# First experts of a two-layer cross-attention and experts kernel: weights of one expert per shared unit, places right behind the choice, unbroken scatters, second product's low halves on VectorE

## Chip, cores and metric
One core of a Trainium2 chip. The metric is device time in microseconds of one launch; the time of before is the median of three runs. One launch was also profiled.

## The reference, cut
x is 16 sequences of 112 tokens of 256 floats. Four steps follow one another: cross-attention of layer 0, the experts of layer 0, cross-attention of layer 1, the experts of layer 1. The change is in the experts of layer 0 alone. With h = layernorm(x), N = 1792 tokens:
```python
gates = softmax(xf @ router_w)                    # 14 experts
top_v, top_i = top_k(gates, 2)
masked = zeros_like(gates).at[arange(N)[:, None], top_i].set(top_v)
masked = masked / (masked.sum(-1, keepdims=True) + EPS)
routed = vmap(_ffn)(rms_w, w1, w2)                # _ffn: silu((rmsnorm(xn)*rw) @ W1) @ W2
shared = vmap(_ffn)(rms_w_s, w1_s, w2_s).sum(0)   # 2 shared experts, for all tokens
x = x + tanh(g_ffn[0]) * (einsum('end,ne->nd', routed, masked) + shared)
```
W1 is 256x512, W2 512x256, float32.

## The kernel before, in words
`build` (L2371) calls the four stages, with a barrier of all engines between them. The stage in question is `l0_experts` (L905). Products in float32 are made of three in bfloat16 (`three_products`, L45): each operand is split into a high half (the cast) and a low half (what the cast lost).

**Units.** The stage runs 57 units (`Unit0`, L890). Units 0 to 15 are shared ones: 8 per shared expert, each with 224 tokens. Units 16 to 56 are 41 blocks of 128 routed tokens. TensorE does for iteration s (from -2): the transposes of block s+2 (`turned`), the first product of unit s+1 (`up`), the second product of unit s (`down`). ScalarE makes the silu from PSUM to `hf` (`silu`, L1184), VectorE the high half `hh` (L1330) and the low half `hl` (L1332) in `halves`, and for shared units the addition to `xs` (`add_shared`, L1334, 2 instructions). `hf` is one buffer: the next silu waits for `h_lo`. `down` waits for `h_lo`.

**Weights.** 16 loads (`LOADS`): the two shared experts, then the 14 routed ones, each of w1 and w2, 512 KB (128x1024 float32) each, through two raw buffers, issued in order on SP (`load`, L988). Load n's w1 waits for the w1 low half of load n-2 (`w1_lo`), its w2 for the w2 low half of load n-2 (`w2_lo`). ScalarE makes the high halves (w1: `split1`, L1152, two instructions with the norm's weight; w2: `high2`, L1161), VectorE w1's low half (`split1`, L1248, two instructions), GpSimd w2's (`split2`, L1023). Load 15 takes the slot of shared expert 0, so it is split when that expert's units are done, in iteration 12, its w2 all on VectorE. Loads 3 to 14 are split in iterations 0 to 5, two in each, behind the unit's work on ScalarE and VectorE.

**Routing.** TensorE makes the logits, VectorE picks the two experts of each token (`choose`, L1272) and, in the same function, the gates. In iteration 3 (`RANK_AT`) TensorE makes ranks (17 matmuls, `ranks`, L1069) and VectorE computes from them each token's place (`place`, L1299, up to `pos_done`) and the expert of each block (`bexp_done`, L1319). GpSimd then issues 32 scatters of 112 rows of 1 KB from `xn` to `xd` in DRAM (L1037). After each five it does the w2 low half of one of loads 9 to 14. SP loads the blocks from `xd` behind all weights and all scatters.

The lines that set this order:
```python
RANK_AT = 3
LAST_AT = 2 * SH - 4
SCATTER_FROM, SCATTERS = 9, 5
...
for n in range(2 * B):
    ...
    if n % SCATTERS == SCATTERS - 1 and ahead:
        split2(ahead.pop(0))
```


## Time and profile before
| | us |
|---|---|
| runs | 1035.86, 1033.06, 1030.75 |
| median | 1033.06 |
| profiled execution, its own time | 1035.79 |
| its span, first to last instruction | 1034.1 |
| busy in it: TensorE, VectorE, ScalarE, GpSimd | 779.9, 629.7, 470.2, 398.8 |
| mean granted TensorE clock | 0.882 of full |

In the rows below PE is TensorE, PEld its weight loads, DVE VectorE, ACT ScalarE, POOL GpSimd, SPq the queue of SyncE. Times are us from the start of the span unless a column is marked otherwise. The same line stands for all calls of a helper: L51 is the matmul of `three_products`. A name on the left of `<-` is written, those on the right are read. "[4.15 <-DVE f_hl L1332]" means that the engine was idle for 4.15 us before and that this instruction of VectorE ended it. "x2" merges two neighbours of the same kind, and the duration is then that of both.

### The profile page before, as it was taken

How to read it: one execution, taken by the hardware profiler on the slowest of the kernel's cores; microseconds unless marked ns; L12 is line 12 of the kernel's file. 1: busy time of each engine (PE TensorE's matmuls, PEld its weight loads, DVE VectorE, ACT ScalarE, POOL GpSimd, SP SyncE). 2: the span in 40 equal slices, each digit the busy share in tenths (PEclk: the TensorE clock that was granted, in tenths of full speed). 3: DMA queues.
4: the chain of work that ended last, by engine and by line, in shares of the span. 5: the costliest groups of instructions: out<-in, count | busy, mean ns of one | idle time of the engine just before them, and what ended most of it. 6: DMA issues, size and time to landing. Idle time of an engine off the chain costs nothing. (4 is left out here: it accounts for less than half of the span.)

```text
span 1034.1 us, 22027 instructions
## 1 busy us (share of the span) xinstructions
PE 779.9 (75%) x7078; PEld 612.3 (59%) x7093; DVE 629.7 (61%) x1486; ACT 470.2 (45%) x974; POOL 398.8 (39%) x423
## 2 busy tenths in 40 slices
PE   4589999998874866269999999447778627999850
PEld 2357677666563766269877777336667614666430
DVE  8567677776638778446433343157687626666766
ACT  3736555565542654312333333134555315776642
POOL 4377233323200236850000000356687342856555
PEclk9889999999977598779999999779788758999985
DMA  5456223222612345530222222528743021422323
GB/s 151 104 135 162 55 62 76 60 68 46 191 44 83 123 127 173 181 125 7 62 63 64 72 63 67 134 78 223 194 136 91 23 61 50 135 77 86 94 82 102
DMA packets 86021, 101.59 MB, mean 98 GB/s; under 512 B 16854, under 2 KB 72710, under 8 KB 85926
## 3 DMA queue, kind: packets, MB, share of 16 engines
q1 hardware_dynamic: 70614, 69.71, 23.4%
q0 software_dynamic: 12272, 28.81, 10.1%
q10 hardware_dynamic: 3040, 1.81, 0.7%
q8 instruction: 59, 0.97, 0.4%
q14 instruction: 36, 0.29, 0.1%
HBM read 61.03 MB, written 24.38 MB: 83 GB/s over the span
## 5 line engine op out<-in xcount | busy, mean ns | idle before, releaser
L640 DVE TENSOR_REDUCE a_mx<-ps 112x2 f32<-112x750 f32 x128 | 119.8, 936 | 43.7 <-PE ps L323 38.6
L51 PE MATMUL ps<-f_w2hi,f_hh 128*128 (+1 forms) x292 | 83.8, 287 | 44.5 <-DVE f_hl L1332 44.5
L1582 POOL DMA_INDIRECT a_yg<-f_yd,pos x32 | 32.9, 1028 | 210.6 <-POOLq L89 202.0
L1330 DVE CAST f_hh<-f_hf 128x512 bf16<-128x512 f32 (+1 forms) x57 | 32.3, 566 | 109.1 <-ACT f_hf L1188 84.4
L529 ACT ACTIVATE a_Pf<-ps 125x672 f32<-125x672 f32 x128 | 89.9, 729 | 17.1 <-PE ps L271 16.3
L51 PE MATMUL ps<-f_w2hi,f_hl 128*128 (+1 forms) x292 | 83.4, 286 | 0.0
L51 PE MATMUL ps<-f_w2lo,f_hh 128*128 (+1 forms) x292 | 83.4, 286 | 0.0
L323 PE MATMUL ps<-a_stkK,a_stkQ 96*112 96x375 bf16 x256 | 68.1, 349 | 19.8 <-DMA a_stkK<-a_KS 10.0
L51 PE MATMUL ps<-f_xgThi,f_w1hi 128*128 128x128 bf16 x328 | 73.7, 227 | 7.5 <-issue 5.0
L51 PE MATMUL ps<-f_xgTlo,f_w1hi 128*128 128x128 bf16 x328 | 70.6, 217 | 0.0
L51 PE MATMUL ps<-f_xgThi,f_w1lo 128*128 128x128 bf16 x328 | 70.3, 217 | 0.2
L546 POOL DMA_DIRECT2D a_stkK<-a_KS x96 | 51.3, 541 | 45.8 <-DVE a_KS L607 28.7
L2177 ACT ACTIVATE f_rf<-ps,f_ln 128x128 f32<-128x128 f32 x136 | 54.4, 451 | 30.2 <-PE ps L2130 30.2
L51 PEld LDWEIGHTS ps<-f_w2hi,f_hh 128*128 128x128 bf16 (+1 forms) x292 | 34.9, 119 | 51.8 <-DVE f_hl L1332 45.5
L540 POOL TENSOR_TENSOR a_ctxL<-a_ctxF,a_ctxH 128x750 bf16<-128x750 f32 x16 | 25.6, 1602 | 102.9 <-ACT a_ctxH L429 102.9
L2231 POOL TENSOR_TENSOR f_rl<-f_rf,f_rh 128x512 bf16<-128x512 f32 x34 | 39.5, 1160 | 66.8 <-DVE f_rh L2299 65.4
L271 PE MATMUL ps<-a_stkQ,a_stkK 98*125 98x224 bf16 (+1 forms) x384 | 61.2, 269 | 2.3 <-DMA a_stkQ<-a_cneg 2.3
L1188 ACT ACTIVATE f_hf<-ps 128x512 f32<-128x512 f32 x41 | 24.5, 597 | 77.1 <-PE ps L51 77.1
L284 PE MATMUL ps<-a_Pf,a_V 125*32 125x112 f32 x1536 | 52.9, 272 | 2.7 <-DVE xn L655 1.0
L323 PEld LDWEIGHTS ps<-a_stkK,a_stkQ 96*112 96x112 bf16 (+1 forms) x256 | 29.8, 133 | 41.7 <-issue 22.1
L271 PEld LDWEIGHTS ps<-a_stkQ,a_stkK 98*125 98x125 bf16 x384 | 47.8, 142 | 9.3 <-DMA a_stkQ<-a_cneg 2.5
L1027 POOL TENSOR_TENSOR f_w2lo<-f_raw,f_w2hi 128x1024 bf16<-128x1024 f32 x15 | 34.8, 2326 | 45.6 <-ACT f_w2hi L1164 45.5
(398 smaller groups left out, 2454.9 us busy)
## 6 DMA issues: line engine op xcount, KB each, us to landing
f_raw<-F_w SPq DMA_DIRECT2D x28, 512.0 KB
f_xg<-f_xd SPq DMA_DIRECT2D x75, 128.0 KB
f_yd<-f_yo SPq DMA_DIRECT2D x75, 128.0 KB
a_ctxF<-ctxT SPq DMA_DIRECT2D x16, 375.0 KB
a_cT<-ctxT SPq DMA_DIRECT2D x16, 375.0 KB
a_cR<-ctx SPq DMA_DIRECT2D x16, 375.0 KB
f_xd<-a_zero POOLq DMA_DIRECT2D x1, 5248.0 KB, 19.8
a_stkK<-a_KS SPq DMA_DIRECT2D x96, 46.9 KB
```

Of the source, the lines that this page charges most:

```text
L51: ins = nc.tensor.matmul(out, l, r, start=first and i == 0, stop=last and i == len(steps) - 1)
L271: last = nc.tensor.matmul(psST[:C, j % 2, c, :QW], stkK[:, b.slot, j // JJ, j % JJ, c * C:(c + 1) * C], stkQ[:, bass.ds(b.b, 1), j // JJ, ...
L284: last = nc.tensor.matmul(psPV[VW * q:VW * (q + 1), :], V[:, b.slot, c, h, :], Pf[:, h // 2 % PB, c, h % 2 * T:(h % 2 + 1) * T], start=c = ...
L323: last = nc.tensor.matmul(psMX[:T, h, :S], stkQ[0:96, bass.ds(n.b, 1), j // JJ, j % JJ, h * T:(h + 1) * T].rearrange("p o q -> p (o q)"), ...
L529: nc.scalar.activation(Pf[:, s % PB], psST[:C, s % 2, :SC, :QW], ACT.Exp).then_inc(exp_done, 1)
L546: pool.dma_start(stkK[32 * a:32 * a + 32, w.slot, :, jj, :], KS[32 * jj:32 * jj + 32, w.odd, part])\
L640: nc.vector.reduce_max(mx[:, n.odd, 2 * j:2 * j + 2], psMX[:T, :, :S], AX).then_inc(mx_red, 1)
L1027: nc.gpsimd.tensor_tensor(w2[1][:, l.slot], raw2[:, i], w2[0][:, l.slot], ALU.subtract).then_inc(w2_lo, 1)
L1330: nc.vector.tensor_copy(hh[:, s.odd, 0:n], hf[:, 0:n]).then_inc(h_hi, 1)
L1582: nc.gpsimd.indirect_dma_start(out=yg[:, i, b, :], out_offset=None, in_=yd, in_offset=bass.IndirectOffsetOnAxis(k.pos[:, i, b:b + 1], 0), ...
L2177: nc.scalar.activation(rf[:, t % 2, i, :], k.ps[:, 2 + t % 2, i * P:(i + 1) * P], ACT.Relu, bias=ln[:, 1, bass.ds(e, 1), i], scale=ln[:, 0 ...
L2231: nc.gpsimd.tensor_tensor(rl[:, t % 2], rf[:, t % 2], rh[:, t % 2], ALU.subtract).then_inc(r_lo, 1)
```

## The change
- Loads 3 to 15 are split one in each of iterations 0 to 12, and not two in each of 0 to 5 and the last in 12.
- `ranks` runs in iteration 0, between `up` of unit 1 and `down` of unit 0. On VectorE gates and places are computed in iteration 0, ahead of unit 1's halves; load 2's w1 low half stands behind them and no longer ahead of the choice. The experts of the blocks are computed in iteration 4, in a function of their own.
- GpSimd makes the w2 low halves of loads 0, 1, 2, 13 and 14; VectorE makes those of loads 3 to 12. The 32 scatters stand in one row, between loads 2 and 13.
- The high half of a shared unit's hidden rows moves from VectorE to ScalarE, right behind the silu. Routed blocks keep it on VectorE.

```diff
-        RANK_AT = 3
-        LAST_AT = 2 * SH - 4
-        SCATTER_FROM, SCATTERS = 9, 5
+        RANK_AT, EXPERTS_AT = 0, 4
+        FIRST_LOADS = 3
+        LOW_POOL = (0, 1, 2, 13, 14)
...
             def _(pool):
...
+                    at_least(pool, w2_lo, l.n)
                     nc.gpsimd.tensor_tensor(w2[1][:, l.slot], raw2[:, i], w2[0][:, l.slot], ALU.subtract).then_inc(w2_lo, 1)
-                for l in LOADS[:SCATTER_FROM]:
-                    split2(l)
+                for n in LOW_POOL[:FIRST_LOADS]:
+                    split2(LOADS[n])
...
                 for n in range(2 * B):
...
-                    if n % SCATTERS == SCATTERS - 1 and ahead:
-                        split2(ahead.pop(0))
-                for l in ahead:
-                    split2(l)
+                for n in LOW_POOL[FIRST_LOADS:]:
+                    split2(LOADS[n])
...
             def _(pe):
...
-                    if s == RANK_AT:
-                        ranks()
                     if t is not None:
                         turned(t)
...
                         up(m, expert.get(m.u))
+                    if s == RANK_AT:
+                        ranks()
                     if d is not None:
                         down(d, expert.get(d.u))
...
             def _(act):
...
+                def high(s):
+                    n = HM * s.width
+                    act.wait_ge(act_done, s.u + 1)
+                    at_least(act, y_full, s.u - 1)
+                    nc.scalar.activation(hh[:, s.odd, 0:n], hf[:, 0:n], ACT.Copy).then_inc(h_hi, 1)
...
                         silu(m)
+                        if m.shared is not None:
+                            high(m)
...
-                    if 0 <= s < SH - 2:
-                        for l in LOADS[3 + 2 * s:5 + 2 * s]:
-                            split1(l)
-                            if l.n < len(LOADS) - 1:
-                                high2(l)
-                    if s == LAST_AT:
-                        split1(LOADS[-1])
+                    if 0 <= s < len(LOADS) - FIRST_LOADS:
+                        l = LOADS[FIRST_LOADS + s]
+                        split1(l)
+                        if l.n < len(LOADS) - 1:
+                            high2(l)
...
             def _(dve):
...
                 split1(LOADS[1])
-                split1(LOADS[2])
...
+                def split2(l):
+                    i = l.n % NRAW
+                    dve.wait_ge(w_in2[i], 16 * (l.n // NRAW + 1))
+                    dve.wait_ge(w2_hi, l.n + 1)
+                    dve.wait_ge(w2_lo, l.n)
+                    tt(w2[1][:, l.slot], raw2[:, i], w2[0][:, l.slot], ALU.subtract).then_inc(w2_lo, 1)
...
-                    nc.vector.tensor_copy(hh[:, s.odd, 0:n], hf[:, 0:n]).then_inc(h_hi, 1)
+                    if s.shared is None:
+                        nc.vector.tensor_copy(hh[:, s.odd, 0:n], hf[:, 0:n]).then_inc(h_hi, 1)
...
                     if s == RANK_AT:
+                        gates()
                         place()
+                        split1(LOADS[2])
+                    if s == EXPERTS_AT:
+                        block_experts()
...
-                    if 0 <= s < SH - 2:
-                        for l in LOADS[3 + 2 * s:5 + 2 * s]:
-                            split1(l)
-                    if s == LAST_AT:
-                        split1(LOADS[-1])
-                        split2(LOADS[-1])
+                    if 0 <= s < len(LOADS) - FIRST_LOADS:
+                        l = LOADS[FIRST_LOADS + s]
+                        split1(l)
+                        if l.n < len(LOADS) - 1 and l.n not in LOW_POOL:
+                            split2(l)
+                        if l.n == len(LOADS) - 1:
+                            last2(l)
```
`gates` and `block_experts` are the lines of `choose` from L1290 to L1297 and of `place` from L1313 to L1319; `last2` is the old `split2` of VectorE (L1264).

## Rows read from the trace of the kernel before

**Rows 1.** The page's first line: the span.
```profile
span 1034.1 us, 22027 instructions
```

**Rows 2.** Stretches: busy PE, PEld, DVE, ACT, POOL (count), clock, DMA share, GB/s.
```profile
368.00:447.00 79.00, 39.47 (x340) 38.13 (x338) 53.00 (x64) 31.16 (x40) 55.20 (x37) 0.80 0.54 177
447.00:480.00 33.00, 32.70 (x291) 32.48 (x292) 17.74 (x30) 6.84 (x9) 8.31 (x7) 0.91 0.16 52
...
375.00:385.00 10.00, 7.61 (x80) 7.10 (x77) 6.91 (x9) 6.09 (x8) 3.92 (x2) 1.00 0.87 273
```

**Rows 3.** Waits in 320 to 490 us: total, times, longest.
```profile
PE ps L51 <- DVE f_hl L1332: 44.0, 6, 15.6
```

**Rows 4.** Timeline of TensorE: start, duration, then in brackets the idle time before.
```profile
365.02 0.46 PE L51 MATMUL ps<-f_w2hi,f_hh 128*112 128x256 bf16 x1 [4.15 <-DVE f_hl L1332]
...
377.01 0.27 PE L51 MATMUL ps<-f_w2hi,f_hl 128*112 128x256 bf16 x1
```

**Rows 5.** Timeline of GpSimd: scatters and w2 low halves, first to last.
```profile
399.45 1.08 POOL L1037 DMA_INDIRECT f_xd<-xn,pos  x1 [5.21 <-issue]
...
403.70 3.51 POOL L1037 DMA_INDIRECT f_xd<-xn,pos  x1 [0.30 <-issue]
...
408.48 2.14 POOL L1027 TENSOR_TENSOR f_w2lo<-f_raw,f_w2hi 128x1024 bf16<-128x1024 f32 x1
...
432.67 0.95 POOL L1037 DMA_INDIRECT f_xd<-xn,pos  x1 [0.30 <-issue]
...
455.86 1.11 POOL L1037 DMA_INDIRECT f_xd<-xn,pos  x1 [0.30 <-issue]
```

**Rows 6.** Timeline of the SP queue: the issue of load 11's w2.
```profile
410.65 0.37 SPq L996 DMA_DIRECT2D f_raw<-F_w  x1
```

**Rows 7.** Timeline of ScalarE: a copy, weight splits, two silus.
```profile
344.61 0.92 ACT L1171 ACTIVATE xT_hi<-ps 128x896 bf16<-128x896 f32 x1 [2.23 <-PE ps L1057]
...
380.69 1.33 ACT L1158 ACTIVATE f_w1hi<-f_raw,f_rw 128x512 bf16<-128x512 f32 x2 [0.21 <-DMA f_raw<-F_w]
...
414.72 1.06 ACT L1164 ACTIVATE f_w2hi<-f_raw 128x1024 bf16<-128x1024 f32 x1 [5.03 <-DMA f_raw<-F_w]
...
470.04 0.92 ACT L1190 ACTIVATE f_hf<-ps 128x896 f32<-128x896 f32 x1 [4.00 <-PE ps L51]
474.96 0.92 ACT L1190 ACTIVATE f_hf<-ps 128x896 f32<-128x896 f32 x1 [4.00 <-PE ps L51]
```

**Rows 8.** Timeline of VectorE: choice, gates, places, halves, additions, w1 low halves.
```profile
360.77 0.38 DVE L1290 TENSOR_TENSOR f_xg<-f_pick,f_xg 112x224 f32<-112x224 f32 x1
...
363.00 0.17 DVE L1297 TENSOR_TENSOR gate<-gate,f_top 112x16 f32<-112x16 f32 x1
...
388.30 1.41 DVE L1252 SCALAR_TENSOR_TENSOR f_w1lo<-f_raw,f_rw,f_w1hi 128x512 bf16<-128x512 f32 x2
...
394.71 0.16 DVE L1301 COPY f_cnt<-ps 112x14 f32<-112x14 f32 x1
...
398.26 0.18 DVE L1312 CAST pos<-f_posf 112x32 int32<-112x32 f32 x1
...
400.67 0.61 DVE L1330 CAST f_hh<-f_hf 128x896 bf16<-128x896 f32 x1
401.31 1.09 DVE L1332 TENSOR_TENSOR f_hl<-f_hf,f_hh 128x896 bf16<-128x896 f32 x1
402.32 0.87 DVE L1339 SCALAR_TENSOR_TENSOR xs<-ps,tg_f,xs 112x256 f32<-112x256 f32 x2
403.11 2.73 DVE L1252 SCALAR_TENSOR_TENSOR f_w1lo<-f_raw,f_rw,f_w1hi 128x512 bf16<-128x512 f32 x4
...
434.66 3.60 DVE L1252 SCALAR_TENSOR_TENSOR f_w1lo<-f_raw,f_rw,f_w1hi 128x512 bf16<-128x512 f32 x2 [3.13 <-ACT f_w1hi L1158]
```

**Rows 9.** TensorE, the rank matmuls by their line: durations (ns), starts.
```profile
L1074 PE MATMUL ps<-f_Mb,f_trib x16: 195/218/257, 379.6 to 380.6; 112*112 112x224 bf16 x1, 112*112 112x210 bf16 x1, 112*112 112x196 bf16 x1, 112*112 112x182 bf16 x1
```

**Rows 10.** VectorE, its one w2 low half, by its line (ns).
```profile
L1270 DVE TENSOR_TENSOR f_w2lo<-f_raw,f_w2hi x1: 1226/1226/1226, 480.4 to 480.4; 128x1024 bf16<-128x1024 f32 x1
```

More of the change, by code:

```diff
@@ L1033, in _ @@
                 pool.wait_ge(xn_act, B // 2)
-                ahead = list(LOADS[SCATTER_FROM:-1])
                 for n in range(2 * B):
@@ L1171, in _ @@
                     nc.scalar.activation(k.xT[0][:, :, cols(g)], k.ps[:, bank:bank + 2, :GT], ACT.Copy).then_inc(x_hi, 1)
-                for l in LOADS[1:3]:
+                for l in LOADS[1:FIRST_LOADS]:
                     split1(l)
@@ L1261, in _, with last2 @@
                 split1(LOADS[1])
-                split1(LOADS[2])
-                def split2(l):
+                def last2(l):
                     i = l.n % NRAW
@@ L1289, in choose, with gates @@
                     tt(Mb[:, 0:B, :], pick[:, 0], pick[:, 1], ALU.add).then_inc(mb_done, 1)
+                def gates():
                     link(tt(tmp, pick[:, 1], EX, ALU.mult))
@@ L1312, in place, with block_experts @@
                     nc.vector.tensor_copy(pos[:], posf[:]).then_inc(pos_done, 1)
+                def block_experts():
                     of = cmp[0:1, 0:NBLK * E].rearrange("p (i e) -> p i e", e=E)
```

## The prediction
> **What bounds the kernel now.** I read the page first, then a table of stretches, then the waits of the stage that the diff touches, then each engine's timeline in it. The profiled execution has a span of 1034.1 us [rows 1] and 1035.79 us with what lies around it; the median of the three runs is 1033.06, so 2.7 below it. All sums are made against 1035.79.
>
> The first experts' stage starts at about 326 us, its shared units at 355. Units run at full pace only at the end: in 447 to 480 TensorE is busy nearly throughout, in the 79 us from 368 to 447 only half the time, while GpSimd is busy for 55 us of these [rows 2]. TensorE waits 44.0 us in all for low halves of the hidden rows [rows 3], and the longest such wait is 15.6 us; after one of 4.15 us it comes back at the lower clock, 1.2 GHz: 0.46 us for a matmul that takes 0.27 at 2.4 GHz a few us later [rows 4]. VectorE, which they name, is itself waiting. The chain is: GpSimd makes w2's low half between groups of five scatters [rows 5], that frees a raw buffer, SP issues the next load (410.65) [rows 6], ScalarE has it at 414.72, 4.1 us later [rows 7], and ScalarE does two such loads before it comes to the next silu. A load costs 5 x 1.25 + 2.3 = 8.6 us on GpSimd (scatter 0.95 and 0.30 before it; low half 2.14 and a gap) [rows 5]. TensorE's own pace is 4.92 us a unit (silu to silu, 470.04 to 474.96) [rows 7]. So three units (5, 6 and 7) are spread over six loads of 8.6 us. What ends last is the preparation of weights, in the order that GpSimd gives it.
>
> **The change, part by part.**
> Times below are those of the profile of before, carried forward.
>
> 1. Places early. The choice ends as gates' first step starts, 360.8 [rows 8]. TensorE has finished the first products of units 0 and 1 by then (365.02 less 4.15 idle, 360.9 [rows 4]), as before; its 17 rank matmuls take 1.3 us (379.5 to 380.8) [rows 9], so ranks are there at 362.2. VectorE first makes unit 0's low half: 1.09, to 362.0, since the cast (0.61) is now ScalarE's. Then gates, 2.4 (360.8 to 363.2), to 364.4, and the places, 3.7 (394.7 to 398.4), to 368.1 [rows 8]. Before: 398.4. The places are 30 us earlier.
>
> 2. w1's low half of load 2 moves behind the places: 1.41 [rows 8], to 369.5. It used to lie in time that VectorE spent waiting for logits. SP's queue feels it: load 4's w1 waits for it, and is issued at 369.5 where it was issued at 354.8. Unit 1's low half ends at 370.6. TensorE has been idle since 367.2 (362.2 and one unit's 4.92: unit 0's second product, unit 2's first), 3.4 us. After 4.15 us idle it came back at the lower clock [rows 4]; I grant the same here, 1.4 us, and it costs nothing, as VectorE is later still.
>
> 3. The unit's work per engine. VectorE: low half 1.09, shared addition 0.87, w1 low 1.41 [rows 8], w2 low 1.23 [rows 10]: 4.60. Were the cast left there, 5.21. ScalarE: silu 0.92, the cast (priced by a copy of 128x896, 0.92), w1 high 1.33, w2 high 1.06 [rows 7]: 4.23. TensorE 4.92. So VectorE limits while it is late, TensorE afterwards. With silu, cast and low half in a row (2.9 us) behind a first product, the second product still starts on time, since TensorE has 2.6 us of the unit before to do. The price of the cast on ScalarE lies between 0.92 and 1.06 (the larger copy) and hides in 0.7 us of slack.
>
> 4. The chain. VectorE at 370.6; then 4.60 for each iteration, and once 2.3 for the block experts, which moved to iteration 4: unit 9's low half starts at 369.5 + 8 x 4.60 + 2.3 = 408.6, and with hand-overs 409.3. From there TensorE is the limit: unit 10's first product starts at 409.3, unit 13's at 424.1, and unit 13's silu at 426.5. It was 474.96 [rows 7]. That is 48.5 us earlier, and what follows (three more units, 41 blocks, two more stages) has the same work.
>
> 5. Weights. In iteration s load s+3 is wanted by ScalarE 1.9 us after unit s+1's first product ends (silu and cast). Its buffer was released two units (9.84) before that iteration's own w1 low half, which ends 5.4 after the product (2.0 to the low half, then 1.09, 0.87, 1.41): 1.9 + 9.84 - 5.4 = 6.3 us between release and want. The landing takes 4.1 [rows 6, 7], so 2 us are covered. What can take it away is DMA: a unit now moves 1.05 MB of weights and 3.9 scatters of 115 KB, 1.5 MB in 4.92 us, 305 GB/s; the densest stretch of before moved 273 GB/s at a DMA share of 0.87 [rows 2], so about 314 would be full. The bounds are nothing and, if full means 275, 0.55 us for each of the 8 units under scatters, 4.4 us. I take 2.
>
> 6. Scatters. 32 of them ran in 57.5 us with six low halves of 2.14 between: 1.40 each, stalls included [rows 5]. Starting 1 us behind the places, 369.1 + 45 = 414. GpSimd's last low halves (loads 13, 14) are wanted from 420.9 on. So nothing waits. The limit is 1.8 us each. Load 15's w2 is wanted at 431.9 (unit 13's 426.5 and the 5.4 of step 5), so issued at 427.8, behind load 13's low half, which then starts at 425.6: (425.6 - 369.1) / 32.
>
> 7. GpSimd's two low halves against VectorE. Two w1 low halves took 3.60 instead of 1.41 when GpSimd worked beside them [rows 8]. That can happen in iterations 10 and 11: up to 4.4 us on VectorE, less 1.8 by which its low half is ahead of TensorE: between 0 and 2.6. I take 2.5, as GpSimd starts those just when VectorE does the same load's w1.
>
> 8. The casts removed from VectorE's queue (0.61 each [rows 8]) are in step 3. The routed blocks keep theirs. Nothing else is touched.
>
> Sum: -48.5 + 2 + 2.5 = -44. 1035.8 - 44 = 991.8 for a profiled execution; as the median is 2.7 below, 989 to 992. I say 991.
>
> **The rivals.**
> A. Scatters starved by VectorE. One scatter took 3.51 us [rows 5]; it began while VectorE ran four w1 low halves in a row (403.11 to 405.84), behind them a cast [rows 8], and ended 0.8 us after the cast. If a scatter gets through only in a true gap of VectorE, then in the new order w1 low, w2 low and the next low half stand together for 3.7 us, and one scatter passes in a unit where VectorE limits, two where TensorE does. Laid against step 4's times, 12 or so are done at 405 and the 32nd, helped by VectorE's own wait at load 15, at 444. GpSimd's two low halves start there, the first ends at 446, load 15's w2 lands at 450, VectorE splits it until 452.1, and through unit 14's low half (453.2), unit 15's silu and cast, unit 15's low half starts at 455.2; in step 4 it was 438.2. That is 17 us, and 1.4 for the clock: gain 44 less 18, 26, or 1007 against the median. Against it: the mean is 1.40 us, 3.51 is the longest of 32. The Trainium skill (SBUF — State Buffer, section "Who interferes with whom") has it that a VectorE instruction with two SBUF inputs contends with a GpSimd instruction that reads SBUF, the second blocked until the first finishes; it also infers that writing descriptors needs the write side, which such an instruction leaves free. By the first this rival holds, by the second step 6; the row of 3.51 us speaks for the first.
> B. DMA full. If landings grow past 6.3 us under scatters, units there take about 5.8 us, not 4.92: 8 x 0.9 = 7 us beyond step 5, about 998. For it: the sum of bytes. Against it: the loads issued during scatters landed in 4.1 us [rows 6, 7], the scatters then as dense as they will be.
> C. Slower. The scatter of 3.51 us was also the fourth of an unbroken run, and the kernel of before never runs more than five. If what stops it is the number outstanding, each further one costs 3.51 + 0.30: 32 x 3.8 = 122, to 491 where it was 457. Load 13's low half ends at 493, w2 of load 15 lands at 497 and is split by 499, unit 15's low half starts at 502, where it was at 486.5 (474.96 + 9.84 + 1.7): 15.6 later, and 1.4 for the clock, so 17 us slower, 1050. It decides from about 3.3 us a scatter on. Against it: the fifth followed at once (57.5 us in all) [rows 5], and five in a row came four more times.
> That the change doesn't do what it says I exclude: the places depend on the ranks alone, and these on the choice.
>
> **How the numbers follow.** Forecast 0.65, A 0.18, B 0.12, C 0.05. What a measurement can tell from no change is 0.5%, 5 us. All but C are faster by more. Faster 0.94, same 0.01, slower 0.05. The range: below, no losses in steps 5 and 7, 1033.1 - 48.5 = 984.6, and 1 less for the hand-overs granted, 983.5; above, A's 1007 and a little: 1008.
>
> **What would show it.** Right: scatters from about 369 to 414 at 1.3 to 1.5 us each; places at 368; VectorE over 90% busy from 363 to 425; TensorE at full clock from 375 on with gaps under 1 us; unit 13's silu near 429; low-half waits of TensorE near 6 us instead of 44. A: scatters of 2 to 4 us each in w1 and w2 low halves, and a TensorE gap at unit 14's second product. B: ScalarE waiting for raw weights in each unit at a DMA share near 1. C: scatters of 3.5 us whatever VectorE does. The forecast is wrong if silu of unit 13 comes after 440, or if the routed blocks, which nothing touches, take another time.

## The result, and the profile after

The changed kernel took 1001.24 us (median of 4 runs, 998.6 to 1002.66), the kernel before 1031.9 beside it (4 runs, 1030.2 to 1035.86): a ratio of 0.9695, 95% interval 0.9658 to 0.9731. The forecast of 991 was 10 us too low, inside its range of 983.5 to 1008. The profiled execution took 1002.12 us where that of before took 1035.79: 33.7 gained, 44 forecast.

The page's first line and its group of scatters, of the changed kernel (duration of one in ns, then idle time before):

```profile
span 1000.4 us, 22043 instructions
...
L1037 POOL DMA_INDIRECT f_xd<-xn,pos x32 | 61.4, 1919 | 24.8 <-issue 24.8
```

Stretches of the changed kernel, columns as in [rows 2]:

```profile
368.00:380.00 12.00, 9.30 (x73) 9.22 (x74) 10.62 (x17) 6.70 (x9) 9.44 (x4) 0.86 0.69 222
380.00:390.00 10.00, 10.00 (x100) 9.98 (x99) 9.38 (x14) 8.24 (x12) 8.78 (x5) 1.00 0.76 248
...
410.00:420.00 10.00, 10.00 (x100) 9.98 (x98) 8.48 (x13) 8.24 (x11) 8.78 (x5) 1.00 0.86 269
...
430.00:440.00 10.00, 4.37 (x43) 4.12 (x40) 2.10 (x4) 1.87 (x2) 7.87 (x8) 0.82 0.27 81
440.00:450.00 10.00, 3.01 (x16) 2.50 (x17) 3.34 (x5) 0.38 (x1) 4.73 (x3) 0.50 0.37 122
```

From 380 to 420 TensorE is busy throughout at full clock, where before it was busy half the time [rows 2]. That part of the forecast came true. Then comes what was not forecast: 20 us in which TensorE is busy for 7.4. In the first half of them GpSimd is busy for 7.87 us of 10, with scatters, and each other engine for less than half of the time.

Waits of the changed kernel between 320 and 470 us (total, times, longest):

```profile
PE ps L51 <- DVE f_hl L1347: 3.2, 1, 3.2
PE ps L1080 <- DMA f_xg<-f_xd: 12.6, 1, 12.6
...
DVE f_w2hi L1271 <- DMA f_raw<-F_w: 14.5, 1, 14.5
...
ACT f_w1hi L1156 <- DMA f_raw<-F_w: 0.6, 1, 0.6
```

The 44.0 us for low halves [rows 3] have shrunk to 3.2. In their place stand two waits that [rows 3] don't have, for data that come by DMA: VectorE's for w2 of load 15, and TensorE's for the first routed block's rows. Unit 15's silu starts when TensorE releases it (row at 451.28 below), and TensorE's first product of unit 15 stood behind the transposes of the block whose rows came last; load 15's w2 would have held the unit 1.7 us less (VectorE's low half of unit 14, behind it, ended at 449.57). The timelines show what both waits hang on. ScalarE, the silus of units 13 and 15 (start, duration, idle time before):

```profile
426.87 0.92 ACT L1188 ACTIVATE f_hf<-ps 128x896 f32<-128x896 f32 x1 [0.85 <-PE ps L51]
...
451.28 0.92 ACT L1188 ACTIVATE f_hf<-ps 128x896 f32<-128x896 f32 x1 [3.17 <-PE ps L51]
```

GpSimd, from the last scatters on:

```profile
438.27 0.95 POOL L1037 DMA_INDIRECT f_xd<-xn,pos  x1 [0.30 <-issue]
439.53 0.95 POOL L1037 DMA_INDIRECT f_xd<-xn,pos  x1 [0.30 <-issue]
440.51 2.13 POOL L1028 TENSOR_TENSOR f_w2lo<-f_raw,f_w2hi 128x1024 bf16<-128x1024 f32 x1
```

And SP's queue behind it:

```profile
442.66 0.37 SPq L996 DMA_DIRECT2D f_raw<-F_w  x1
443.07 4.96 SPq L1005 DMA_DIRECT2D f_xg<-f_xd  x4
```

Read them from the bottom up. Load 15's w2 is issued 0.02 us after GpSimd has made load 13's low half, which starts as the last scatter ends, 440.5. The block's rows are issued behind w2. Unit 13's silu came 48.1 us earlier than before (474.96 [rows 7], now 426.87); unit 15's came 33.7 earlier (485.02, now 451.28), and 33.7 is what the whole launch gained, so nothing changed behind it. The 14.4 between the two are the scatters' lateness, the lower clock behind the stall with it: 0.50 granted from 440 to 450.

**What makes a scatter long.** GpSimd in the steady part:

```profile
406.52 2.94 POOL L1037 DMA_INDIRECT f_xd<-xn,pos  x1 [0.30 <-issue]
409.77 1.37 POOL L1037 DMA_INDIRECT f_xd<-xn,pos  x1 [0.31 <-issue]
```

VectorE beside it, consecutive:

```profile
405.31 0.87 DVE L1354 SCALAR_TENSOR_TENSOR xs<-ps,tg_f,xs 112x256 f32<-112x256 f32 x2
406.10 1.41 DVE L1256 SCALAR_TENSOR_TENSOR f_w1lo<-f_raw,f_rw,f_w1hi 128x512 bf16<-128x512 f32 x2
407.42 1.22 DVE L1280 TENSOR_TENSOR f_w2lo<-f_raw,f_w2hi 128x1024 bf16<-128x1024 f32 x1
409.22 1.09 DVE L1347 TENSOR_TENSOR f_hl<-f_hf,f_hh 128x896 bf16<-128x896 f32 x1 [0.58 <-ACT f_hh L1195]
```

The first scatter ends at 409.46, the two low halves of weights at 408.64: 0.82 behind. The second ends at 411.14, the low half of the hidden rows at 410.31: 0.83 behind. A scatter that no such work holds takes 0.95. The longest, 3.94, began at 393.26 and ended 0.83 behind a run that ended at 396.37. So in this order a scatter is held until the *whole unbroken run* of w1, w2 and hidden-row low halves (each reads two operands from SBUF) is over, and then needs 0.82 to 0.86 us. Shared additions, which read PSUM and SBUF, hold none, nor does a low half that begins after the scatter has (scatter at 423.74, low half at 423.98: 0.95). Two scatters and a bit pass per 4.92 us unit: (440.48 - 369.64) / 32 = 2.21 us each, gap included.

The changed kernel has one exception, where the block experts follow. GpSimd, and VectorE beside it:

```profile
386.70 2.94 POOL L1037 DMA_INDIRECT f_xd<-xn,pos  x1 [0.30 <-issue]
```

```profile
387.59 1.22 DVE L1280 TENSOR_TENSOR f_w2lo<-f_raw,f_w2hi 128x1024 bf16<-128x1024 f32 x1
388.73 0.74 DVE L1328 TENSOR_TENSOR f_yo<-f_iota,f_incl 1x574 f32<-1x574 f32 x1
```

The scatter ends at 389.64, 0.83 behind the w2 low half (388.81), although the next instruction reads two operands from SBUF too and starts 0.08 before that end. It writes float32, on one partition.

### The profile page after: what moved, and what is told of

Its sections match the earlier page's. It is cut to its first block and busy times, and to the rows that moved or that the text cites. A ratio compares the mean times of both kernels' runs of the same rounds, so it can differ in the third digit from the quotient of the medians.

```text
span 1000.4 us, 22043 instructions
## 1 busy us (share of the span) xinstructions
PE 777.1 (78%) x7078; PEld 610.1 (61%) x7093; DVE 610.9 (61%) x1480; ACT 483.1 (48%) x990; POOL 399.5 (40%) x413
## 3 DMA queue, kind: packets, MB, share of 16 engines
q10 hardware_dynamic: 3040, 1.81, 0.8%
## 5 line engine op out<-in xcount | busy, mean ns | idle before, releaser
L529 ACT ACTIVATE a_Pf<-ps 125x672 f32<-125x672 f32 x128 | 89.9, 729 | 17.3 <-PE ps L271 16.7
L51 PE MATMUL ps<-f_w2hi,f_hh 128*128 (+1 forms) x292 | 80.4, 275 | 3.8 <-DVE f_hl L1347 3.7
L51 PE MATMUL ps<-f_w2lo,f_hh 128*128 (+1 forms) x292 | 80.5, 276 | 0.0
L51 PE MATMUL ps<-f_w2hi,f_hl 128*128 (+1 forms) x292 | 80.3, 275 | 0.0
L1037 POOL DMA_INDIRECT f_xd<-xn,pos x32 | 61.4, 1919 | 24.8 <-issue 24.8
L1345 DVE CAST f_hh<-f_hf 128x512 bf16<-128x512 f32 x41 | 17.5, 428 | 83.8 <-ACT f_hf L1186 83.8
L1347 DVE TENSOR_TENSOR f_hl<-f_hf,f_hh 128x512 bf16<-128x512 f32 (+1 forms) x57 | 45.8, 803 | 11.2 <-ACT f_hh L1195 9.8
## 6 DMA issues: line engine op xcount, KB each, us to landing
f_xg<-f_xd SPq DMA_DIRECT2D x75, 128.0 KB, 2.3
f_yd<-f_yo SPq DMA_DIRECT2D x75, 128.0 KB, 1.7
a_ctxF<-ctxT SPq DMA_DIRECT2D x16, 375.0 KB, 3.4
a_cT<-ctxT SPq DMA_DIRECT2D x16, 375.0 KB, 7.2
a_cR<-ctx SPq DMA_DIRECT2D x16, 375.0 KB
```

The lines of the kernel that those rows point to most:

```text
L51: ins = nc.tensor.matmul(out, l, r, start=first and i == 0, stop=last and i == len(steps) - 1)
L529: nc.scalar.activation(Pf[:, s % PB], psST[:C, s % 2, :SC, :QW], ACT.Exp).then_inc(exp_done, 1)
L1037: nc.gpsimd.indirect_dma_start(out=xd, out_offset=bass.IndirectOffsetOnAxis(pos[:, i, b:b + 1], 0), in_=k.xn[:, b, :], in_offset=None, bou ...
L1347: tt(hl[:, s.odd, 0:n], hf[:, 0:n], hh[:, s.odd, 0:n], ALU.subtract).then_inc(h_lo, 1)
```

## The experiments

The stage begins at 321 to 331 us, by what the stage ahead of it took in that execution. So the table counts from the stage's first instruction on GpSimd (its iota, at 326.2 in the changed kernel). "Scatters": start of the first to end of the last, and that divided by 32. The last columns are silus; block 0 is the first routed one. Ratios are against the kernel before on the same chip.

| kernel | median us | ratio, 95% | scatters | unit 13 | unit 15 | block 0 |
|---|---|---|---|---|---|---|
| before | 1031.9 | | 73.6 to 131.1, 1.80 | 149.1 | 159.2 | 163.3 |
| changed | 1001.24 | 0.9695, 0.9658 to 0.9731 | 43.4 to 114.3, 2.21 | 100.6 | 125.1 | 129.2 |
| e1_low_all | 1003.54 | 0.9684, 0.9638 to 0.9731 | 43.4 to 117.4, 2.31 | 100.7 | 126.2 | 131.0 |
| e2_gaps | 988.13 | 0.9542, 0.9486 to 0.9599 | 43.4 to 96.2, 1.65 | 100.9 | 111.0 | 115.2 |
| e3_adds_between | 989.32 | 0.9533, 0.9498 to 0.9567 | 43.4 to 99.7, 1.76 | 100.6 | 110.7 | 114.9 |
| e4_cast_back | 1001.64 | 0.9657, 0.9608 to 0.9706 | 44.1 to 111.9, 2.12 | 102.4 | 123.6 | 128.0 |
| e5_best | 989.14 | 0.9531, 0.9506 to 0.9556 | 45.2 to 99.6, 1.70 | 97.6 | 111.3 | 115.7 |
| e6_places_late | 1010.35 | 0.9725, 0.9687 to 0.9762 | 60.7 to 120.7, 1.88 | 102.1 | 131.3 | 135.5 |
| e7_two_loads | 1012.06 | 0.9752, 0.9723 to 0.9780 | 43.4 to 100.7, 1.79 | 121.9 | 132.0 | 136.2 |
| e8_pool_low | 1005.42 | 0.9683, 0.9657 to 0.9710 | 44.1 to 114.5, with low halves | 116.9 | 126.3 | 130.5 |
| e9_best_lowall | 988.53 | 0.9524, 0.9497 to 0.9551 | 44.7 to 99.4, 1.71 | 97.1 | 107.4 | 111.8 |
| e10_best_gaps | 989.66 | 0.9535, 0.9499 to 0.9571 | 45.1 to 94.9, 1.55 | 99.5 | 111.1 | 115.5 |

The kernel before had medians of 1040.16 beside e1 to e4, 1037.9 beside e5 to e8 and 1037.16 beside e9 and e10; so compare ratios, not medians, across these groups.

### e1_low_all: is it the wait for w2, or the scatters?

Loads 13 and 14 lose their low halves on GpSimd, so that load 15's w2 waits for nothing there:

```
-        LOW_POOL = (0, 1, 2, 13, 14)
+        LOW_POOL = (0, 1, 2)
```

> Edit: VectorE makes the w2 low halves of loads 13 and 14 too, so nothing of the weights waits for GpSimd's scatters. Theory L (a scatter is held as long as VectorE runs instructions with two SBUF inputs back to back; it gets through in the next gap or beside another kind): scatters stay at 2.2 to 2.4 us each and end at 441 to 447. Load 15's w2 then comes in time (VectorE's wait of 14.5 us for it goes), but the blocks' rows are issued behind the last scatter, so TensorE still stands before the first block's transposes, some 7 to 11 us instead of 12.6: 996 to 1000 us against the 1001 of the change. Rival W (the weights of load 15 were the wait, the scatters only beside it): the stall goes nearly whole, 988 us. Rival Q (scatters are slow because of the queue and the DMA traffic, not because of VectorE): as L.

Measured: no gain (0.9684; changed 0.9695), where my theory expected 996 to 1000 us, a miss. VectorE's wait for w2 is gone, and TensorE's stands where it stood. TensorE's wait and SP's issue in e1_low_all:

```profile
PE ps L1080 <- DMA f_xg<-f_xd: 13.8, 2, 12.9
```

```profile
440.15 3.06 SPq L1005 DMA_DIRECT2D f_xg<-f_xd  x4
```

The rows of block 0 may be read only when all rows are scattered, and the last scatter ends 117.4 us into the stage, 438.6 in this execution, 1.6 ahead of that issue. The chain through load 13's low half was one of two that hang on the last scatter; cut, the other takes the same time. That the wait for w2 was itself the cause is refuted. The scatters took 2.31 us each here, within what was expected.

### e2_gaps: the same work with true gaps in it

VectorE waits for its own semaphore between a load's w1 and w2 low halves, and again before the next low half of hidden rows. No work is added or taken away:

```
                 def split2(l):
                     i = l.n % NRAW
+                    dve.wait_ge(w1_lo, l.n + 1)
...
+                    if 1 <= s <= 12:
+                        l = LOADS[FIRST_LOADS + s - 1]
+                        if l.n < len(LOADS) - 1 and l.n not in LOW_POOL:
+                            dve.wait_ge(w2_lo, l.n + 1)
                     if m is not None:
                         halves(m)
```

> Edit: no work changed; VectorE waits on its own semaphore between a load's w1 low half and its w2 low half, and between the w2 low half and the next unit's low half, so that each starts only when the one before has ended. Theory L: a scatter is held for one piece of 1.1 to 1.4 us at most, mean spacing 1.9 us instead of 2.2, the last scatter ends near 430 instead of 440, and the stall of TensorE before the first block shrinks from 12.6 to some 4 us: 991 to 993 us. VectorE loses 0.1 us for each gap. Rival P (the lock is given away at each instruction's end anyway): scatters unchanged at 2.2, time 1001 to 1003. Rival Q (queue or DMA traffic): unchanged too.

Measured: 988.13, ratio 0.9542, whose interval doesn't touch the changed kernel's; better than the 991 to 993 expected, since the scatters fell to 1.65 us each and not 1.9. In the stage, block 0 comes 14.1 us earlier. The scatters of e2_gaps in one row (ns, min/median/max), and of the changed kernel:

```profile
L1037 POOL DMA_INDIRECT f_xd<-xn,pos x32: 951/1105/1942, 366.0 to 417.2; - x32
```

```profile
L1037 POOL DMA_INDIRECT f_xd<-xn,pos x32: 952/1732/3942, 369.6 to 439.5; - x32
```

The gaps themselves are hardly to be seen. VectorE of e2_gaps, consecutive:

```profile
408.74 1.41 DVE L1256 SCALAR_TENSOR_TENSOR f_w1lo<-f_raw,f_rw,f_w1hi 128x512 bf16<-128x512 f32 x2
410.28 1.23 DVE L1281 TENSOR_TENSOR f_w2lo<-f_raw,f_w2hi 128x1024 bf16<-128x1024 f32 x1
411.54 1.09 DVE L1348 TENSOR_TENSOR f_hl<-f_hf,f_hh 128x896 bf16<-128x896 f32 x1
```

Its GpSimd beside it:

```profile
409.30 1.68 POOL L1037 DMA_INDIRECT f_xd<-xn,pos  x1 [0.30 <-issue]
411.28 1.06 POOL L1037 DMA_INDIRECT f_xd<-xn,pos  x1 [0.30 <-issue]
```

408.74 + 1.41 = 410.15, and the next instruction starts 0.13 later; in the changed kernel it starts 0.09 *before* the end that the profile gives (406.10 + 1.41 = 407.51, next 407.42). The scatter of 1.68 ends at 410.98, 0.83 behind the w1 low half, and that of 1.06 at 412.34, 0.83 behind the w2 low half. So the hold ends at the end of an instruction if a pause follows.

This kernel also settles the DMA question further than the changed one could. A stretch of e2_gaps:

```profile
400.00:420.00 20.00, 20.00 (x197) 19.95 (x196) 17.75 (x25) 17.40 (x22) 16.39 (x13) 1.00 0.92 302
```

302 GB/s at a share of 0.92, TensorE without a gap. With denser traffic than in the changed kernel and the same row of scatters, these took less time: rival Q, the queue or the DMA traffic as what makes a scatter long, falls.

### e3_adds_between: other work in the place of the gap

If a gap releases, so should an instruction that doesn't hold. The two shared additions are parted: one goes between the w1 and the w2 low half.

```
-                        add_shared(d)
+                        add_shared(d, (0,) if split else (0, 1))
...
                         split1(l)
...
+                        add_shared(d, (1,))
                         if l.n < len(LOADS) - 1 and l.n not in LOW_POOL:
                             split2(l)
```

> Edit: the second of the two shared additions (one input from PSUM, one from SBUF) is put between a load's w1 and w2 low halves; the same instructions in another order. Theory L with additions that hold nothing: runs of two-SBUF-input work are cut as by gaps, spacing 1.9 us, last scatter near 430, 990 to 993 us. If only a true gap lets a scatter through (L', the additions hold it as well or are too short), spacing stays 2.2 and the time 1001. Rival Q: unchanged, 1001.

Measured: 989.32, ratio 0.9533, just under the 990 to 993 expected; the scatters took 1.76 us each. Scatters and VectorE of e3_adds_between:

```profile
L1037 POOL DMA_INDIRECT f_xd<-xn,pos x32: 955/1410/2226, 368.9 to 423.5; - x32
```

```profile
409.90 1.41 DVE L1256 SCALAR_TENSOR_TENSOR f_w1lo<-f_raw,f_rw,f_w1hi 128x512 bf16<-128x512 f32 x2
411.23 0.48 DVE L1354 SCALAR_TENSOR_TENSOR xs<-ps,tg_f,xs 112x256 f32<-112x256 f32 x1
411.62 1.21 DVE L1280 TENSOR_TENSOR f_w2lo<-f_raw,f_w2hi 128x1024 bf16<-128x1024 f32 x1
```

No gap anywhere, each instruction starts 0.08 or 0.09 before the end of the one ahead, and yet the scatter of this moment (410.73, 1.41) ends at 412.14, 0.83 behind the w1 low half. An addition with an operand in PSUM ends the hold as a gap does. So it is not VectorE's being busy that holds a scatter, but the kind of its instruction. That what counts is where the operands lie isn't shown: the addition also writes float32, where the low halves write bfloat16, and the instruction at 388.73 in the changed kernel, which let a scatter through with both operands in SBUF, writes float32 as well.

### e4_cast_back: does the cast on ScalarE bring anything?

```
-                        if m.shared is not None:
-                            high(m)
...
-                    if s.shared is None:
-                        nc.vector.tensor_copy(hh[:, s.odd, 0:n], hf[:, 0:n]).then_inc(h_hi, 1)
+                    nc.vector.tensor_copy(hh[:, s.odd, 0:n], hf[:, 0:n]).then_inc(h_hi, 1)
```

> Edit: one part of the change undone: the high half of shared units goes back to VectorE (0.61 us each, with a short gap behind it). VectorE's work for a unit rises from 4.6 to 5.2 us, over TensorE's 4.92, so the units are paced at about 5.3 us and VectorE is late by up to 12 x 0.4 = 5 us at unit 13. Theory L: scatters have no idle time of VectorE left, but the gap behind each cast lets one through in every unit: spacing near 2.2 to 2.5, last scatter 441 to 450. The stall at the first block hides VectorE's lateness: 1001 to 1010 us. Rival Q: scatters as before at 2.2, time 1001 to 1003.

Measured: 0.9657, not to be told from 0.9695. GpSimd of e4_cast_back:

```profile
409.25 0.96 POOL L1037 DMA_INDIRECT f_xd<-xn,pos  x1 [0.30 <-issue]
410.52 3.34 POOL L1037 DMA_INDIRECT f_xd<-xn,pos  x1 [0.30 <-issue]
```

VectorE beside it:

```profile
411.27 1.22 DVE L1278 TENSOR_TENSOR f_w2lo<-f_raw,f_w2hi 128x1024 bf16<-128x1024 f32 x1
412.41 0.62 DVE L1342 CAST f_hh<-f_hf 128x896 bf16<-128x896 f32 x1
413.06 1.09 DVE L1344 TENSOR_TENSOR f_hl<-f_hf,f_hh 128x896 bf16<-128x896 f32 x1
```

The cast, though it has but one input, lengthens the run: the scatter that began at 410.52 ended at 413.86, 0.83 behind the cast (413.03) and not behind the w2 low half ahead of it (412.49). But behind the cast VectorE truly pauses, 0.03 us, and then one scatter in two passes in 0.95. Unit 13 is 1.8 later, with 0.6 more per unit on VectorE; the scatters end 2.4 earlier, and block 0 comes 1.2 earlier, too little for these runs to tell in the whole. So this part of the change brought nothing by itself while scatters set the end.

### e5_best: the choice's neighbours put back as well

On e3's order: load 2's w1 low half ahead of the choice again, unit 1's low half between gates and places (which was to spare TensorE the 3.2 us wait), the block experts in iteration 13.

```
-        RANK_AT, EXPERTS_AT = 0, 4
+        RANK_AT, EXPERTS_AT = 0, 13
...
                 split1(LOADS[1])
+                split1(LOADS[2])
...
                         gates()
+                        halves(m)
                         place()
-                        split1(LOADS[2])
```

> Edit on top of the order with one shared addition between the w1 and the w2 low half: load 2's w1 low half stands ahead of the choice again, unit 1's low half ahead of the places instead of behind them, and the experts of the blocks are computed in iteration 13 instead of 4. Theory L and the chain of TensorE: the wait of 3.2 us for unit 1's low half goes and some 1.5 us of it comes back as a wait for unit 2's; scatters end near 424 as in the order without these moves; silu of the first block 2 to 3 us earlier than 440.4: 982 to 985 us where the plain reordering gave 985.35 profiled. If VectorE's queue were the limit and not TensorE (step 4 of the prediction), the moves only shift its work and the time stays at 985 to 989.

Measured: 0.9531 beside e3's 0.9533. Unit 13 is 3.1 us earlier than in e3, and nothing of it is left at unit 15 (block 0 was expected 2 to 3 us earlier, a miss). It is given back where GpSimd makes the low halves of loads 13 and 14 at 422.90 and 425.21. VectorE of e5_best:

```profile
422.92 3.09 DVE L1348 TENSOR_TENSOR f_hl<-f_hf,f_hh 128x896 bf16<-128x896 f32 x1 [1.72 <-ACT f_hh L1195]
...
426.32 2.89 DVE L1256 SCALAR_TENSOR_TENSOR f_w1lo<-f_raw,f_rw,f_w1hi 128x512 bf16<-128x512 f32 x2
```

3.09 for 1.09 and 2.89 for 1.41, 3.5 us together. This is the clash of step 7: absent in the changed kernel, where VectorE is idle when GpSimd gets to these, and there as soon as the scatters are on time. The block experts, moved to iteration 13, stand behind it on VectorE.

### e6_places_late: the choice's early places undone

```
-        RANK_AT, EXPERTS_AT = 0, 4
+        RANK_AT, EXPERTS_AT = 3, 4
...
                 split1(LOADS[1])
+                split1(LOADS[2])
...
                         place()
-                        split1(LOADS[2])
```

> Edit: one part of the change undone: ranks, gates and places in iteration 3 as before (load 2's w1 low half ahead of the choice as before), all else as changed. Theory L: places at 386 instead of 368, scatters held by VectorE until its splits end at 434, some 14 of them left then, last one near 452 instead of 440, load 15's w2 and the first block's rows 11 us later: 1010 to 1014 us. Rival: the scatters are so long hidden that early places bring little (they overlap the same free time at the end): 1001 to 1004.

Measured: 1010.35, within what was expected, ratio 0.9725, whose interval overlaps the changed kernel's, so the size is read from the stage. In the stage block 0 is 6.3 us later than in the changed kernel. The first scatter is 17.2 later, the last only 6.4: 1.88 us each and not 2.21, since the last ones fall into the time in which VectorE waits and passes them at 0.95.

### e7_two_loads: the loads in fewer, longer runs

VectorE and ScalarE make two loads in each of iterations 0 to 5, and load 15 at 12:

```
+        def loads_at(s):
+            return LOADS[3 + 2 * s:5 + 2 * s] if 0 <= s < 6 else LOADS[-1:] if s == 12 else []
...
-                    if 0 <= s < len(LOADS) - FIRST_LOADS:
-                        l = LOADS[FIRST_LOADS + s]
+                    for l in loads_at(s):
```

> Edit: one part of the change undone: loads 3 to 14 in iterations 0 to 5 again, two in each, VectorE making both low halves; places early, scatters unbroken. VectorE has 9.2 us... of work per unit there: 0.87 + 1.09 + 2 x 2.64 = 7.2 against TensorE's 4.92, so TensorE loses about 14 us over six units at waits for low halves, part of it at the lower clock. Theory L: up to about 415 the scatters get through once in 7.2 us, about eight of them; then VectorE is light and the rest need 24 x 1.26 = 30, the last at 443 to 446. Load 13's low half is then late for load 15 by little: silu of the first block 455 to 460, 1002 to 1008 us. If the one load per unit is what frees TensorE and the scatters don't matter (rival W), 1013 or more is expected, as the 14 us come on top of the change.

Measured: 1012.06, ratio 0.9752, a miss for my theory's own 1002 to 1008. I had the scatters end at 443 to 446; they ended at 428.5, at 1.79 each, since VectorE itself stood waiting between its doubled loads and let them through; six got through between two instructions of VectorE with no pause in the record (the one from 381.57 to 384.50 ends 0.83 behind a w2 low half, and the next load's w1 low half starts 0.08 before that one's end). The loss is elsewhere. TensorE's waits in e7_two_loads:

```profile
PE ps L51 <- DVE f_hl L1349: 17.5, 6, 3.6
```

Six waits of 3 us, one for each doubled load; ScalarE also waited 16.7 us in all for raw weights, where it waited 0.8 in the changed kernel; unit 13 is 21 us later than in the changed kernel, and there is no stall at block 0. So longer runs don't always mean slower scatters: what counts is where VectorE lets them through, and here TensorE paid for it.

### e8_pool_low: w2's low halves back on GpSimd, one behind each three scatters

```
-        LOW_POOL = (0, 1, 2, 13, 14)
+        LOW_POOL = tuple(range(15))
...
+                    if n % 3 == 2:
+                        split2(LOADS[3 + n // 3])
-                for n in LOW_POOL[FIRST_LOADS:]:
+                for n in LOW_POOL[FIRST_LOADS + 10:]:
```

> Edit: one part of the change undone: all w2 low halves on GpSimd, one after every three scatters; VectorE makes none. A load costs GpSimd 3 x 1.26 + 2.3 = 6.1 us, over TensorE's 4.92, so units 1 to 11 are paced by it, unit 13's silu comes at 438 to 442 instead of 426.9, but scatters end at about 432 and the stall at the first block is gone or small. Theory L also has VectorE's w1 low halves take 2 to 3.6 us beside GpSimd's subtractions. Together 999 to 1008 us: moving the low halves to VectorE brought nothing net in the change as it stands, since what it gave the units it took from the scatters. Rival: GpSimd's low halves are cheap beside scatters and VectorE's relief counts, 988 to 992.

Measured: 1005.42, ratio 0.9683, within what was expected and not to be told from the changed kernel's 0.9695. GpSimd in e8_pool_low, one turn:

```profile
407.52 2.13 POOL L1028 TENSOR_TENSOR f_w2lo<-f_raw,f_w2hi 128x1024 bf16<-128x1024 f32 x1
409.82 0.96 POOL L1037 DMA_INDIRECT f_xd<-xn,pos  x1 [0.17 <-POOL f_w2lo L1028]
411.09 0.95 POOL L1037 DMA_INDIRECT f_xd<-xn,pos  x1 [0.30 <-issue]
412.34 1.65 POOL L1037 DMA_INDIRECT f_xd<-xn,pos  x1 [0.30 <-issue]
414.01 2.14 POOL L1028 TENSOR_TENSOR f_w2lo<-f_raw,f_w2hi 128x1024 bf16<-128x1024 f32 x1
```

A turn takes 6.5 us and paces the unit, where TensorE's own pace is 4.92; ten low halves and 32 scatters are through at 114.5, as the 32 scatters alone are in the changed kernel (114.3). GpSimd had lost ten instructions of 2.14 to VectorE, and VectorE's longer runs took as much from its scatters. The third named part of the change brought nothing, as it stands; with a break in the run it brings some 15 us in the stage (block 0 at 130.5 here, 115.2 and 114.9 in e2 and e3).

### e9_best_lowall and e10_best_gaps: the rest of what was given back

e9 is e5 with e1's edit; e10 is e5 with e2's waits.

> Edit: e5's moves, and VectorE makes all w2 low halves from load 3 on. In e5 unit 13's silu came 97.6 us after the stage's start, 3.0 earlier than with the plain reordering (100.6), but unit 15's came 0.6 later (111.3 against 110.7): the 3 us were given back at load 15, whose w2 waits for load 13's low half on GpSimd behind the last scatter. Theory L, with that low half on VectorE nothing of the weights waits for GpSimd: unit 15's silu at 107.5 to 108.5, first block's at 112, the launch 3 us shorter than e5 (0.950 of before against 0.953). Rival: VectorE, with 1.2 us more in iterations 10 and 11, is late for TensorE by as much, 0.953 again.

> Edit: e5's moves with the addition between, and in addition the waits on VectorE's own semaphores of e2. Theory L: runs of two-SBUF-input work are one instruction kind long, the last scatter ends 3 us earlier than in e5 (96 us after the stage's start instead of 99.6), load 13's low half and so load 15's w2 too: unit 15's silu at 108 to 110, 0.951 to 0.952 of before. VectorE loses about 0.2 us a unit, which it has only where TensorE limits. Rival: the gaps' cost on VectorE outweighs, as between e2 and e3 (stage to first block 115.15 and 114.89): 0.953 or more.

Measured: 0.9524 and 0.9535. For e9 unit 15 came at 107.4 and block 0 at 111.8, as expected; e10 missed its 0.951 to 0.952 and its 108 to 110 for unit 15, which came at 111.1. In the stage e9's block 0 is the earliest of all, 111.8, by 3.1 us against e3. The expectation laid what was left at load 15 to the wait for w2; the rows of e5 above show the clash with GpSimd instead, and e9 removes both. In the whole launch e9 can't be told from e2, e3, e5 and e10 (their intervals all overlap). e10 has the fastest scatters, 1.55 each, and gains nothing by them: the last one is through 4.7 us earlier than in e5, and GpSimd's two low halves still clash with VectorE's work (two hidden-row low halves of 1.81 and 2.45 us for 1.09). Any of these versions beats both kernels: e9's 0.9524 is another 1.8% under the changed kernel's 0.9695.

## Why the prediction was right and wrong

- **Step 1, right.** Places were cast at 368.14 to 368.32, forecast 368.1. e6 confirms that the earlier places are worth something, but at 6.3 us in the stage far less than the 17.2 by which its first scatter comes later (30 in the kernel before), since the scatters behind them are slow: in e6 each took 1.88, in the changed kernel 2.21.
- **Step 2, right in its sizes, wrong in "it costs nothing".** TensorE was idle for 3.18 us (forecast 3.4). It came back near full clock and fell to the lower one (0.50 granted, 1.2 GHz) 0.9 us later, until 375.0. TensorE in the changed kernel, and the stretch of 372 to 373:

```profile
370.69 0.32 PE L51 MATMUL ps<-f_w2hi,f_hh 128*112 128x256 bf16 x1 [3.18 <-DVE f_hl L1347]
...
372.23 0.42 PE L51 MATMUL ps<-f_w2lo,f_hh 128*112 128x256 bf16 x1
```

```profile
372.00:373.00 1.00, 1.00 (x7) 1.00 (x6) 1.00 (x3) 0.63 (x1) 1.00 (x1) 0.50 1.02 379
```

  Its matmuls started 0.21 us apart there and not 0.11: some 1.6 us, where 1.4 was granted. TensorE set the pace from here on (step 4), so the loss wasn't hidden behind VectorE.
- **Step 3, right.** The cast on ScalarE took 0.95 (0.92 forecast). TensorE's pace is 4.92.
- **Step 4, right in its time, wrong in its engine.** Unit 13's silu came at 426.87, forecast 426.5. But VectorE was not the limit up to 409: it waited about 0.58 us for ScalarE's cast ahead of its low half (row at 409.22), and TensorE was busy in 10.00 of 10.00 us from 380 on. From 371 on TensorE set the pace. VectorE's price was too high: where it had no wait, from 391.05 to 399.54, a unit took 4.25 us and not 4.60, since each instruction starts some 0.08 us before the profile's end of the one ahead.
- **Step 5, term 2 us, measured 0.** ScalarE waited 0.6 and 0.2 us for raw weights in all. The lower bound was right. With e2's 302 GB/s at a share of 0.92 and no loss, rival B falls.
- **Step 6, the step that failed.** "32 of them ran in 57.5 us with six low halves of 2.14 between: 1.40 each, stalls included." It measured 2.21 each, over the "limit of 1.8 each" that the step itself gave, and the last ended at 440.5, not 414. The mean of [rows 5] was taken from a kernel in which VectorE was idle for a third of the time (53.00 busy of 79 [rows 2]) and had at most w1's low halves and a cast in a run; the change fills these pauses and lays w1's, w2's and the next low half end to end. The price of 1.40 belonged to VectorE's old order, not to the scatter. With the measured price the step's own rule gives a stall of 14.2 (369.1 + 32 x 2.21 = 439.8, where 425.6 was the limit); unit 15's silu came at 451.28 where step 4 has 436.3 (426.5 and two units of 4.92), 15.0. The step asked only for load 15's w2. The wait that ended last was TensorE's for block 0's rows, which hang on the last scatter too and stand in no step.
- **Step 7, term 2.5 us, measured 0 in the changed kernel** (GpSimd's two low halves took 2.13 and 2.12, VectorE idle), and real at 3.5 us in e5.
- **The sum**: -48.5 + 0 + 0 + 15.0 = -33.5; measured -33.7. That the forecast missed by only 10 us is in part luck: 4.5 us charged in steps 5 and 7 and not paid stood against the 15.0 of step 6, and the range held the result because it had been drawn out to rival A's time.
- **Rival A was what happened**, in mechanism and nearly in size: last scatter at 444 (440.5), unit 15's low half at 455.2 (453.31), gain 26 (33.7). The difference is the 4.5 us of steps 5 and 7, which it had also charged, and its stall of 18.4 where 15.0 came, the scatters being 3.5 us faster than its count of one in a unit where VectorE limits. It deserved more than 0.18: the row of 3.51 us was the only one of before that showed a scatter against a long run, which is what the change makes of every unit, and 0.8 us behind the cast's end was its signature. TensorE came back from the stall at the lower clock, as it had said.
- **Rival C** is refuted: the last six scatters of the changed kernel, 433.23 to 440.48, with 26 issued ahead of them, took 0.95 each while VectorE was quiet, and so did ten in a row in e6 (437.42 to 449.70).

The Trainium skill (SBUF — State Buffer, section "Who interferes with whom") says that a VectorE instruction with two SBUF inputs contends with a GpSimd instruction that reads SBUF. This case's traces agree for the low halves: 0.95 grows to 2.94 and 3.94. The same section of the Trainium skill also infers that `tensor_tensor` leaves the writing of descriptors free; that helped no scatter here, but a scatter reads its positions from SBUF as well, so no run here can tell which of the two is held. The Trainium skill speaks of one instruction at a time; what these runs show is mostly a block by a whole run of them.

**Left open.** Why a run without a pause mostly doesn't let GpSimd in between two instructions stays open. In the twelve traces 259 scatters end 0.82 to 0.86 us behind a low half or a cast of VectorE; 18 of these low halves had another instruction with two SBUF operands right behind them, no pause between, and let the scatter in all the same: 8 ahead of the block experts' first instruction, 8 between the two instructions of one w1 low half, 2 between a w2 low half and the next w1's. One scatter of e4 (424.10, 1.95) was held across a pause of 0.37 us. Which part of the change brought most of the gain isn't separated either: block 0 came 34.1 us earlier in the stage, and undoing one part gave back 6.9 us at most (e7), 6.3 in e6, 1.2 in e8 and nothing in e4. Whether one of e2, e3, e5, e9 and e10 is faster than another isn't settled.

## What to carry to other kernels

When a change fills an engine's pauses, ask who lived in them: a duration measured beside a half-idle neighbour is not a price. Take the row in which the neighbour was busiest, ask what it waited for, and lay that against the neighbour's new order, as rival A did; multiplying the longest row would have given 122 us for the scatters, where 70.8 came. Where VectorE makes such low halves beside GpSimd's indirect DMAs, break its queue up with an addition that reads PSUM or a wait for its own semaphore; the work stays the same, and some 14 us in the stage came from it, of a launch of 1001. And when a long wait goes, look which second chain hangs on the same late event before pricing its removal.

## What the runs showed of the hardware that was not expected

- A scatter of 112 rows took 0.95 us on GpSimd with VectorE quiet, and ended 0.82 to 0.86 us behind the end of the VectorE run that held it, whether the run was one low half (1.37), two weight halves (2.94) or a load's two low halves and the hidden rows' one (3.94).
- The hold mostly passes from one VectorE low half to the next (18 of 259 times it didn't, without a pause to be seen), and it ended at a true pause (0.03 us was enough, behind the cast in e4; 0.13 in e2) or at an addition with a PSUM operand between (e3). A cast from f32 to bf16 within SBUF held as the two-input ones did.
- Weights and scatters together moved 302 GB/s at a share of 0.92 without a wait of TensorE, above the 273 GB/s that was the densest before.
